# A six-layer decoder on one core: two convolution taps as diagonal matmuls, sign layer steps halved, another order of steps

## The reference, cut to what matters

```python
x = ln(x + causal_attention(x))              # "self":  softmax, one head of 256
x = ln(x + ln(masked_attention(x, ctx)))     # "cross": softmax, one head of 256
x = ln(x + sign_layers(x))                   # "sign":  256 -> 1024 -> 1024 -> 256, weights +1 or -1, relu
x = ln(x + relu_linear_attention(x))         # "perf":  16 heads, 64 features, causal
x = ln(x + gated_linear_attention(x, ctx))   # "mlstm": 8 heads, exponential gates
h = bit_linear(x, w1)                        # "quant": tokens rounded to 8 bits, weights to -1, 0, 1
h = silu(depthwise_conv1d(h, conv_w, conv_b))  # 3 taps along the tokens, 1024 channels
x = ln(x + bit_linear(h, w2))
```

## Time and profile before

| | |
|---|---|
| median of 3 runs (lowest, highest) | 868.52 us (868.14, 871.88) |
| the profiled execution, its own time | 874.67 us |
| its span, from the first instruction to the last | 873.4 us |
| mean granted TensorE clock | 0.901 of full speed |
| ACT busy | 368.2 us (42%) |
| POOL busy | 147.9 us (17%) |

### The profile page before, as it was taken

One profiled execution on the slowest core, in us unless ns is written; L12 is line 12 of the kernel. 1 busy time (PEld: TensorE's weight loads), 2 busy tenths in 40 slices (PEclk: granted clock), 3 DMA queues, 4 the chain that ended last, 5 costly groups with the idle time before them and its releaser, 6 DMA issues.

```text
span 873.4 us, 14709 instructions
## 1 busy us (share of the span) xinstructions
PE 757.4 (87%) x5872; PEld 531.1 (61%) x5872; DVE 588.3 (67%) x1486; ACT 368.2 (42%) x659; POOL 147.9 (17%) x223
## 2 busy tenths in 40 slices
PE   9999999999999985779889999999999968668214
PEld 5776654575787774676564676676476846547102
DVE  2485864264546779987789856566365767778796
ACT  2564632123314625843338433343354125473183
POOL 5021100031000324102310020110014120113200
PEclk9999999999999995858899999999999968869565
DMA  9501000001000102003000030000000000000001
GB/s 353 189 1 73 1 1 0 1 2 44 8 2 2 26 1 73 25 25 96 1 1 0 2 96 2 2 1 2 1 2 1 2 1 2 0 2 2 0 12 36
DMA packets 12739, 23.75 MB, mean 27 GB/s; under 512 B 768, under 2 KB 7040, under 8 KB 12416
## 3 DMA queue, kind: packets, MB, share of 16 engines
q1 hardware_dynamic: 12672, 22.82, 7.6%
HBM read 20.72 MB, written 2.10 MB: 26 GB/s over the span
## 4 chain that ended last, share of the span: by engine, by line
PE 71%; DVE 20%; POOL 3%; issue 3%; ACT 2%; DVEq 0%; ACTq 0%
PE bank L719 13%; PE bank L543 7%; PE bank L535 5%; PE bank L567 5%; PE bank L588 5%; PE bank L810 3%; PE bank L729 3%; PE bank L792 3%; PE bank L707 2%; PE bank L760 2%; POOL small L2071 2%; DVE work L1630 2%; PE bank L1011 2%; DVE work L1624 2%; DVE stats L1121 1%
## 5 line engine op out<-in xcount | busy, mean ns | idle before, releaser
L2001 POOL TENSOR_TENSOR rstd<-rstd,minus_half 128x2 f32<-128x2 f32 x56 | 44.5, 795 | 458.7 <-DVE rstd L1127 458.5
L719 PE MATMUL bank<-work,f0w 128*128 128x512 f16 x512 | 112.8, 379 | 0.0
L719 PEld LDWEIGHTS bank<-work,f0w 128*128 128x128 f16 x512 | 50.1, 98 | 59.4 <-issue 0.8
L1337 DVE SCALAR_TENSOR_TENSOR work<-bank,work 128x512 f16<-128x512 f32 x64 | 42.2, 686 | 45.0 <-ACT work L1829 44.8
L1829 ACT ACTIVATE work<-bank 128x512 f16<-128x512 f32 x64 | 36.6, 596 | 74.8 <-PE bank L719 60.5
L588 PE MATMUL bank<-work 128*128 128x256 f32 x208 | 49.8, 382 | 0.0
L2071 POOL TENSOR_TENSOR small<-small,minus_half 128x8 f32<-128x8 f32 x16 | 27.7, 1729 | 105.2 <-DVE small L1560 105.2
L1011 PE MATMUL bank<-work 128*128 128x66 f32 (+1 forms) x256 | 36.8, 307 | 8.7 <-DVE work L1501 6.2
L1011 PEld LDWEIGHTS bank<-work 128*128 128x128 f32 x256 | 36.6, 227 | 10.3 <-issue 7.3
L588 PEld LDWEIGHTS bank<-work 128*128 128x128 f32 x208 | 37.4, 190 | 5.1 <-issue 0.8
L810 PE MATMUL bank<-work 64*128 64x128 f32 x512 | 38.7, 292 | 1.1 <-DVE work L1420 1.1
(11 more groups left out here) (296 smaller groups left out, 1771.4 us busy)
## 6 DMA issues: line engine op xcount, KB each, us to landing
work<-in_mask SPq DMA_DIRECT2D x4, 1024.0 KB, 8.8
xT<-in_xT SPq DMA_DIRECT2D x4, 512.0 KB, 5.2
ctxT<-in_ctxT SPq DMA_DIRECT2D x4, 512.0 KB, 5.9
perf_w<-in_k SPq DMA_DIRECT2D x3, 512.0 KB, 11.3
perf_w<-in_perf_w SPq DMA_DIRECT2D x1, 1536.0 KB, 6.0
ctx<-in_w SPq DMA_DIRECT2D x2, 512.0 KB, 14.0
work<-in_w SPq DMA_DIRECT2D x1, 1024.0 KB, 16.0
x<-in_x SPq DMA_DIRECT2D x2, 512.0 KB, 15.2
```

The lines of the kernel that those rows point to most:

```text
L719: ins = nc.tensor.matmul(u.bank[:, :], f0w1[:, k, m * P:(m + 1) * P], s.h1[part][:, k, :], start=(k == 0 and part == 0), stop=(k == NF - 1 ...
L1337: low_part(what, m, dst, number + m, lambda o, x, hi: nc.vector.scalar_tensor_tensor(out=o, in0=x, scalar=0.0, in1=hi, op0=ALU.max, op1=AL ...
L2001: nc.gpsimd.tensor_tensor(s.rstd[:, two], s.rstd[:, two], minus_half[:, 0:2], ALU.pow).then_inc(s.rstd_made.sem, 1)
```

## The change

Three things change. First, the order of the steps on all five engines. In round 1 stream a now runs ahead: PE takes stream a through both attentions nearly alone, stream b's attentions lie beside a's sign layer and `perf`, b's sign layer beside a's `perf`, and b's `perf` beside a's `mlstm` and `quant`. From the second sign layer of stream a in round 2 up to `quant` the order is nearly that of before. The loads are reordered to fit. Second, every `sign.b` step on PE is split in two of 8 matmuls, so that a step of the other stream can stand between the halves. Third, in round 2 of each stream the first and the middle tap are made by PE: two fp32 matmuls of 512 columns against 128 x 128 diagonal matrices that hold the tap weights, accumulated in a PSUM bank (step `quant.taps j`, placed behind `hidden j+1`). DVE then adds the third tap to that bank in one instruction, ACT's instruction for the middle tap goes, and the bias moves into Silu. The diagonals are made once on POOL, in the place of the sign weights, after `sign.b7` of both streams in round 2. On POOL's queue this stands behind a's `mlstm.weigh` and ahead of b's `sign.rstd0`.

`claim` waits for a bank and could issue constant matmuls for the entries of `KEEP`; `KEEP` is empty, so it only waits.

```diff
 TURNS = {
     "tensor":
-        "a1 b1 a2 b3 a2 b1 a2 b1 a3 b1 a1 b2 a3 b4 a1 b1 a3 b3 a2 b2 a2 b3 a1 b5 a1 b5 a4 b1 a2 b2 a2 b3 a1 b7 a1 b1 "
...
-        "a1 b1 a1 b21 a2 b16",
+        "a8 b1 a4 b1 a6 b2 a2 b1 a13 b3 a1 b4 p1 a2 b1 a3 b2 a4 b1 a2 b1 a1 b1 a6 b1 a2 b1 a4 b1 a4 b2 a3 b1 a2 b2 a2 "
...
+        "b1 a1 b10 a1 b1 a1 b2 a1 b1 a2 b3 a2 b1 a1 b1 a1 b2 a1 b2 a6 b1 a1 b1 a1 b1 a1 b1 a1 b2 a1 b19 a2 b23",
...
     "gpsimd":
...
+        "a7 b3 a5 b4 a4 b2 a1 b2 a1 b1 a5 b1 a2 b3 a2 b2 a2 b1 a1 b4 a1 b1 a2 b1 a4 b2 a2 b3 a1 b4 a4 w1 b1 a1 b4 a5 "
+        "b1 a2 b12 a2 b2",
     "sync":
-        "w1 a1 w1 b1 w2 a1 w2 b1 w1 b2 a2 w1 a1 b1 a1 b1 a2 b2 a3 b3 a2 b2",
+        "w2 a2 w4 b1 a1 w1 a1 b3 w1 a2 b1 a4 b2 a1 b4 a2 b2",
 }
+KEEP = {}
...
+    taps = f0w1[:, :, :].rearrange("p k n -> p (k n)").bitcast(F32)[:, 0:NF * 2 * P].rearrange("p (j k n) -> p j k n", j=NF, k=2)
...
         for j in range(NF):
             s.banks.use(("quant", n, "hidden", j))
+            if n == ROUNDS - 1 and j > 0:
+                s.banks.use(("quant", n, "taps", j - 1))
+        if n == ROUNDS - 1:
+            s.banks.use(("quant", n, "taps", NF - 1))
...
+        def claim(s, n, name, u):
+            pe.wait_ge(*u.free)
+            for _ in range(KEEP.get(f"{name} {s.index} {n}", 0)):
+                pe.wait_ge(constants_by_gpsimd, 5)
+                nc.tensor.matmul(u.bank[:, :], identb[:, :], bar_upper[:, :, :].rearrange("p a b -> p (a b)"), start=True, stop=True)
...
                 for k in range(NF):
+                    if k == NF // 2:
+                        yield f"sign.b{m}.2"
                     pe.wait_ge(*s.banks["sign", n, "a", k].read)
...
+            def two_taps(j):
+                u = s.banks["quant", n, "taps", j]
+                claim(s, n, f"quant.taps{j}", u)
+                pe.wait_ge(*taps_made.at(0))
+                pe.wait_ge(*s.edges.at(n))
+                pe.wait_ge(*s.banks["quant", n, "hidden", j].read)
+                for k in range(2):
+                    ins = nc.tensor.matmul(u.bank[:, :], taps[:, j, k, :], s.flat[j % 4][:, k:k + T], start=(k == 0), stop=(k == 1))
+                ins.then_inc(u.filled, 1)
...
             def convolve(j):
                 i = j % 4
+                if last:
+                    u = s.banks["quant", n, "taps", j]
+                    dve.wait_ge(*u.full)
+                    nc.vector.scalar_tensor_tensor(out=s.hid[:, j, :], in0=s.flat[i][:, 2:T + 2], scalar=conv_w[:, j, 2:3],
+                                                   in1=u.bank[:, :], op0=ALU.mult, op1=ALU.add).then_inc(u.emptied, 1)
+                    return
...
-                if j < NF:
+                if j < NF and n < ROUNDS - 1:
...
+                        ins = nc.scalar.activation(s.hid[:, j - 1, :], s.hid[:, j - 1, :], ACT.Silu, bias=conv_b[:, j - 1:j])
...
+        def weights():
+            yield "quant.taps"
+            for each in streams:
+                pool.wait_ge(*each.banks["sign", ROUNDS - 1, "b", NF - 1].full)
+            for j in range(NF):
+                ins = nc.gpsimd.tensor_tensor(taps[:, j, :, :], ident[:, :].unsqueeze(1).broadcast_to([P, 2, P]),
+                                              conv_w[:, j, 0:2].unsqueeze(2).broadcast_to([P, 2, P]), ALU.mult)
+            ins.then_inc(taps_made.sem, 1)
```

More of the change, by code:

```diff
@@ L562, in scores @@
                 barred = slice(width - P if causal else 0, width)
-                pe.wait_ge(*u.free)
+                claim(s, n, f"{name}.score{t}", u)
+                if t == 0:
+                    ready()
                 if not causal:
@@ L572, in turn_t @@
                 u = s.banks[name, n, "turn", t]
-                pe.wait_ge(*u.free)
+                claim(s, n, f"{name}.turn{t}", u)
                 pe.wait_ge(*s.banks[name, n, "score", t].read)
@@ L680, in front_half @@
             yield "sign.xT0"
+            claim(s, n, "sign.xT0", s.banks["sign", n, "xT", 0])
             wait_normed(s, n, 2, 0)
@@ L754, in front_half @@
                     four = [s.banks["perf", n, c, kind, j] for j in range(PAIRS)]
+                    claim(s, n, f"perf.{kind}.{c}", four[0])
                     for u in four:
@@ L767, in front_half @@
                 four = [s.banks["perf", n, c, "ft", j] for j in range(PAIRS)]
+                claim(s, n, f"perf.ft.{c}", four[0])
                 for u in four:
@@ L800, in scores @@
                     two = [s.banks["perf", n, c, "masked", 2 * j + i] for i in range(2)]
+                    claim(s, n, f"perf.score{j}.{c}", two[1])
                     for u in reversed(two):
@@ L875, in front_half @@
                 u = s.banks["perf", n, c, "spread"]
-                pe.wait_ge(*u.free)
+                claim(s, n, f"perf.spread.{c}", u)
                 pe.wait_ge(*s.den_inverse.at(n, c))
@@ L908, in back_half @@
             u = s.banks["mlstm", n, "gate"]
-            pe.wait_ge(*u.free)
+            claim(s, n, "mlstm.gate", u)
             for k in range(NC):
@@ L939, in back_half @@
             u = s.banks["mlstm", n, "cols"]
+            claim(s, n, "mlstm.cols", u)
             pe.wait_ge(*s.key_gates.at(n))
-            pe.wait_ge(*u.free)
             pe.wait_ge(*s.gates_final.at(n))
@@ L963, in back_half @@
                 u = s.banks["mlstm", n, "head", h]
-                pe.wait_ge(*u.free)
+                claim(s, n, f"mlstm.head{h}", u)
                 pe.wait_ge(*s.part1.at(n))
@@ L978, in back_half @@
                     place = t * (t - 1) // 2
-                    pe.wait_ge(*u.free)
+                    claim(s, n, f"mlstm.state{t}", u)
                     pe.wait_ge(*s.memory_ones.at(n))
@@ L994, in back_half @@
                     u = s.banks["mlstm", n, "before", t]
-                    pe.wait_ge(*u.free)
+                    claim(s, n, f"mlstm.before{t}", u)
                     pe.wait_ge(*s.banks["mlstm", n, "state", t].read)
@@ L1002, in back_half @@
                 u = s.banks["mlstm", n, "out", t]
-                pe.wait_ge(*u.free)
+                claim(s, n, f"mlstm.out{t}", u)
                 for i in range(2):
@@ L1024, in back_half @@
                 u = s.banks["quant", n, "turn", p]
-                pe.wait_ge(*u.free)
+                claim(s, n, f"quant.turn{p}", u)
                 pe.wait_ge(*s.q1_made.at(n, p))
@@ L1035, in back_half @@
                     u = s.banks["quant", n, "row1"]
-                    pe.wait_ge(*u.free)
+                    claim(s, n, "quant.row1", u)
                     pe.wait_ge(*s.scaled_tokens.at(n, 1))
                     token_row(u, s.back1)
+            last = n == ROUNDS - 1
+            def two_taps(j):
[7 more added lines that the diff above has]
+                ins.then_inc(u.filled, 1)
             for j in range(NF):
                 yield f"quant.hidden{j}"
+                claim(s, n, f"quant.hidden{j}", s.banks["quant", n, "hidden", j])
                 if n == 0:
@@ L1046, in back_half @@
                 project_T(s.banks["quant", n, "hidden", j], f1w1, j * P, s.q1T)
+                if last and j > 0:
+                    yield f"quant.taps{j - 1}"
+                    two_taps(j - 1)
+            if last:
+                yield f"quant.taps{NF - 1}"
+                two_taps(NF - 1)
             yield "quant.topT"
             u = s.banks["quant", n, "topT"]
-            pe.wait_ge(*u.free)
+            claim(s, n, "quant.topT", u)
             pe.wait_ge(*s.compared.all(n))
@@ L1055, in back_half @@
             u = s.banks["quant", n, "row2"]
-            pe.wait_ge(*u.free)
+            claim(s, n, "quant.row2", u)
             pe.wait_ge(*s.scaled_tokens.at(n, 2))
@@ L1075, in back_half @@
                 u = s.banks["quant", n, "down", t]
-                pe.wait_ge(*u.free)
+                claim(s, n, f"quant.down{t}", u)
                 for k in range(NF):
@@ L1622, in hidden @@
                 if j >= 4:
-                    dve.wait_ge(*s.convolved.at(n, j - 4))
+                    dve.wait_ge(*(s.banks["quant", n, "taps", j - 4].read if last else s.convolved.at(n, j - 4)))
+                if last:
+                    dve.wait_ge(*s.edges.at(n))
                 nc.vector.scalar_tensor_tensor(out=s.flat[i][:, 1:T + 1], in0=u.bank[:, :], scalar=f1_scale[:, 0:1],
@@ L1945, in back_half @@
                 if j >= 1:
-                    act.wait_ge(*s.convolved.at(n, j - 1))
-                    nc.scalar.activation(s.hid[:, j - 1, :], s.hid[:, j - 1, :], ACT.Silu).then_inc(s.shaped.sem, 1)
+                    if n < ROUNDS - 1:
+                        act.wait_ge(*s.convolved.at(n, j - 1))
+                        ins = nc.scalar.activation(s.hid[:, j - 1, :], s.hid[:, j - 1, :], ACT.Silu)
+                    else:
+                        act.wait_ge(*s.banks["quant", n, "taps", j - 1].read)
+                        ins = nc.scalar.activation(s.hid[:, j - 1, :], s.hid[:, j - 1, :], ACT.Silu, bias=conv_b[:, j - 1:j])
```

(1 more changed line is left out.)

25 lines of the change are left out of this document (17 added, 8 removed), and 49 rows, old and new, of the table TURNS.

## The result

The changed kernel takes 860.33 us (median of 4 runs, 859.42 to 860.43) beside 868.96 us for the kernel before: a ratio of 0.989, with a 95% interval of 0.9863 to 0.9916. In a second series on another occasion it took 858.9 us (5 runs) beside 870.3. The forecast was 857.0, in a range of 840 to 876. The time came out near the forecast, but the terms did not: those of the order's first part, of its second part and of the sign steps' halves were each wrong by more than 4 us, what the order does after 715 us was not costed at all, and the errors cancelled.

A forecast was written before the change was run, and what follows sets the result against it. PE's work bounds up to 270.2 us, DVE's from there to 465.9, b's chain of steps the end. Order -8.5, halves 0, POOL +1, a's taps -1, b's taps -3: -11.5 from 868.5 gives 857.0 us, range 840 to 876.

The forecast's parts named there:

- First part of the order: Start of a's `mlstm` in round 1 moves by -34 us: 41 of b's PE work comes off, 7 of waits come on.
- Second part, the share: From a's `mlstm` in round 1 to a's `sign.b0` in round 2: DVE stays 82.5% busy, 221 us, +25.5.
- 0, between -2 and +2: Halving the `sign.b` steps moves no end where PE is full: 0 us, bounds -2 and +2.
- No slice of PE at half clock there: Expected sign between a's `mlstm.xT0` in round 1 and a's `sign.b0` in round 2: no PE slice at half clock.
- the slower rival: Chains set the middle's length; DVE's share under 78.4% repays all; at 76%, middle 240 us, kernel 876; chance 0.19.
- POOL: Eight diagonals ahead of b's `sign.rstd0` in round 2 may delay `perf.xT0`: +1 us, bounds 0 and +8.
- a's taps: a's `quant` in round 2: PE taps delay b's chain, less DVE work stands in its way: -1 us, bounds +5.2 and -6.
- b's taps: b's last hidden layer: DVE drops from four instructions to three per period; -3 us in all, bounds -7.5 and +11.
- With PE working without a break it should stay so: b's last hidden layer: PE's clock, full from 829.9 us before, stays full; eight taps and six `hidden` take 16.4 us.
- The better mix: Middle: b's `perf` beside a's `mlstm` raises DVE's share to 88%, 207 us instead of 221, kernel 843; chance 0.24.
- Taps for nothing: No constant matmul is issued and the taps' bank waits cost what they free; only the order counts: 861 us; chance 0.03.
- The rival of the cold taps: b's last hidden layer: taps at half clock, 33 us where the phase had 22, +11, kernel 871; chance 0.07.

## Why the prediction was right, and where it was wrong

The sum said -11.5; the medians moved by -8.6 in the first series and -11.4 in the second.

**First part of the order.** Forecast -34 = -41 + 7 of waits; measured -42.1 (270.20 to 228.11). The 41 were counted rightly. The 7 us of waits did not come, and most of their cover is the sign steps' halves: with whole steps the same landmark moves by -36.0, 6.1 us less. Of these 1.7 are only the second half of b's `sign.b7`, which stands ahead of the landmark there; the other 4.4 are most of the 7. The step that failed is "0, between -2 and +2" for the halves, argued from PE being full. PE was full because short steps had something to stand beside; on this order the halves are worth 11 us (869.98 against 858.9). The row that priced such a wait was weak too: the half clock of the earlier trace rows was there in one execution of before and not in the other.

**Second part, the share.** Forecast 221 us for the middle, +25.5; measured 224.8 against 193.3, +31.5. VectorE's work was 178.2 instead of the 182.5 forecast, and its share 79% instead of 82.5%. The mechanism was right in part: 9.6 us of work added on VectorE moved the end by 10.6, but work added on PE moved it by about half or more of its size. One share for all of the middle was wrong. In the first third it is 72% (58.0 of 81.1), while PE is busy 89%: b's steps that moved there are PE's. And the clock was 0.92: with constants it was 0.99 and the share 82%. "No slice of PE at half clock there" was a sign that I named, and it was not met: the second part had 0.84. The middle ended a point above the share (78.4%) at which the slower rival begins; with the 7 us of waits in the first part the order up to there would have given 3.6 us instead of 10.6.

**The two together** gave -10.6 at a's `sign.b0` in round 2 (463.53 to 452.95), forecast -8.5: near it by two errors of opposite sign, which is luck.

**After 715 us.** I took the order for "nearly that of before" up to `quant` and costed nothing behind it. There, without taps, it loses 8.8 us of 13.2. This was the most costly omission: a's last residual and layer norm, 4.4 us, moved into b's last hidden layer on VectorE's queue, on the chain of the end. The last turns of VectorE's string hold it: `b30 a1 b9 a1 b8` before, `a1 b9 a1 b25` after, so that a's last step, which had stood behind b's hidden layer, now stands in it. The other place, b's gate arithmetic behind a's hidden layer, makes 4.5 of the 8.8.

**POOL.** Forecast +1 out of 0 to 8. The diagonals took 5.5 us and PE waited 0.43 us ahead of b's `perf.xT0`. The second line gives shortest, median and longest of the eight in ns (their mean is 722):

```profile
636.97 5.51 POOL L2154 TENSOR_TENSOR f0w<-ident,columns 128x256 f32<-128x256 f32 x8
L2154 POOL TENSOR_TENSOR f0w<-ident,columns x8: 606/612/1060, 637.0 to 641.9; 128x256 f32<-128x256 f32 x8
638.14 1.12 DVE L1549 TENSOR_TENSOR work<-work 128x512 f32<-128x512 f32 x1
645.00 0.63 PE L541 MATMUL bank<-ident,ctx 128*128 128x128 f32 x4 [0.43 <-DVE ctx L1184]
```

The nearest row, 0.694 us, was the right price on the mean, because it is a mix of the same kind: six of the eight took 0.61 us and two took 1.06. Both of these ran beside VectorE's L1549, which reads two tiles in SBUF and whose first instance took 1.12 us there instead of 0.69. The Trainium skill ("GPSIMD Engine Reference", Key points) says that POOL contends with VectorE's instructions of two SBUF inputs. The trace agrees, but the price stays far from the slow row's, since VectorE had only two such instructions in these 5.5 us. The last diagonal ended at 642.48 us, and the instruction of VectorE that POOL's root waits for (L1175) at 642.50, after 0.58 us where it takes 0.17 elsewhere; so the eight held up the chain by at most 0.4 us there.

**a's taps.** Forecast -1, measured -4.9 in the medians (taps in a alone against none) and -2.3 in the traces of after and of no taps (b's `quant.hidden0` at 814.10 instead of 816.37). By the medians the end I called "all of DVE's", -6, was the nearer one, by the traces the forecast; which holds stays open. The mechanism is seen in both: b's gate chain waits for a's hidden layer on VectorE, and PE had the room, 25.1 us of unbroken work at full clock from 716.4 on.

**b's taps.** Forecast -3 with the phase at 21.5 us; the phase was 23.4 and 23.0, longer than or equal to that of before, and yet its taps were worth 3.8 us (3.6 in the traces: 23.0 against 26.6). Two steps failed. "With PE working without a break it should stay so": the kernel after has its clock at 0.55 in the first 5.8 us, and 1.87 us are lost on the first pair (columns as in the stretches above):

```profile
814.20:820.00 5.80, 5.67 (x10) 2.11 (x10) 2.97 (x8) 0.56 (x1) 0.69 (x1) 0.55 0.00 0
820.00:826.00 6.00, 6.00 (x18) 2.44 (x17) 5.63 (x12) 3.98 (x6) 0.00 (x0) 1.00 0.00 0
```

With constants ahead the phase was 21.5. And the phase had the norm in it, which before had not. That `topT` would be quicker was right (0.63 us instead of 1.09); `row2` was not (1.91, since PE had waited 3.13 and 1.40 us). The reading of PSUM cost nothing again (744 ns beside 752 with both inputs in SBUF), against the figure of the Trainium skill ("VectorE: DVE Perf Modes", The TRN2 errata).

**The rivals.** The better mix (88%) did not come, nor did the slower middle. "Taps for nothing", 0.03, was the worst of the chances: the rival that was nearly true is its opposite, that the order gives little without the taps (2.7 us, halves included). Nor does it give anything without the halves (0.4 us, taps included). What the order gives with neither was not run. The rival of the cold taps set 33 us against 22, the window of the earlier trace rows; the phase it speaks of took 23.1, so its price was 10 and not 11. So the total was met by luck: order, halves and diagonals, forecast at -7.5, gave -2.7, and the taps, forecast at -4, gave -8.6.

## What to carry to other kernels

Read an order written by hand to its last turn, on every queue: work of the other stream that moves into the phase that sets the end counts nearly in full (4.4 us of it made that phase 3.5 us longer here), and an instruction taken out there is worth what stands ready to use its room. A step with many matmuls is best cut where an engine's short step must be answered, since PE looks full either way (in the 100 us up to a's `mlstm` in round 1 it is 97% busy with whole steps and 99% with halves). Where PE's gaps are 1 to 5 us and the rows behind them run at the half clock, fill them with constant matmuls sized to the gap and no larger: 150 of them were worth 15 us here, and 44 in the wrong size nothing.

## What was not expected of the hardware

The half clock cost more than I expected of a stretch that I had put down to VectorE: in the middle 7.8 us (224.8 to 217.0) for a mean clock of 0.92 against 0.99, with the same work on VectorE. A constant matmul of 512 columns took 0.23 us at full clock and 0.44 us at the half, so a gap holds half as many if PE comes to it cold (16 and 12 of them, with all constants, with and without taps):

```profile
424.24 3.62 PE L534 MATMUL bank<-bar_upper,identb 128*128 128x512 bf16 x16
811.98 5.30 PE L538 MATMUL bank<-bar_upper,identb 128*128 128x512 bf16 x12 [1.07 <-DVE work L1682]
```

The Trainium skill ("TensorE: Matmul & The Clock Gate", Part 1) says that activity releases the throttle. The rows agree: b's `turn1` took 0.63 us in the kernel after, behind PE's waits, and 0.39 in the kernel with the fitted constants ahead of it.

The executions of one kernel differ by more than 0.5%: before took 865.4 to 875.0 us in one series. Behind the same wait of 2.7 us the same step ran at a granted clock of 0.50 in one execution of before and of 1.00 in another, and the two traces differed by 2.0 us from 421 to 466 us. So a wait in one trace does not tell what the step behind it will cost in the next execution.
